# The phase ahead of the selective scans: transposes of delta*u relabelled to the next slot, dt broadcast by a one-row matmul, buffers and waits placed anew

## The chip, the core and the metric

The kernel runs on one core of a Trainium2 chip. The metric is the device time of one execution in microseconds. Before the change three runs took 3381.05, 3383.88 and 3386.18 us; the median is 3383.88 us.

## What is computed

A two-layer decoder over x of 4 batches x 512 tokens x 256 channels. Only the start of layer 0 matters here, a Mamba block on the normalised input, followed by attention, cross-attention and mixtures of experts that the change does not touch:

```python
def mamba_block(x, ...):                      # x: (4, 512, 256), already layer-normed
    residual = x
    xn = rmsnorm(x, norm_m_w)
    x_ssm, z = split(xn @ in_proj_w.T)        # 512 channels each
    x_ssm = silu(causal_depthwise_conv4(x_ssm) + conv_b)
    ssm_p = x_ssm @ x_proj_w.T                # 33 columns: B (16), C (16), dt (1)
    Bp, Cp, dt_raw = ssm_p[:16], ssm_p[16:32], ssm_p[-1:]
    delta = softplus(dt_raw @ dt_w.T + dt_b)  # 512 channels from one column
    A = -exp(A_log)
    y = selective_scan(x_ssm, delta, A, Bp, Cp, D_skip)   # 16 states, over 512 tokens
    return residual + (y * silu(z)) @ out_proj_w.T
```

## The kernel before

Five engines run their own instruction lists and meet at semaphores: PE (matmul), DVE (vector), ACT (scalar functions), POOL (GpSimd) and SP, which issues most DMAs. The order on each engine is written out by hand. SBUF is one tensor, `arena`, so the profile names nearly every buffer `arena`; buffers are laid over one another by `take(..., at=...)`.

Ahead of the main loop over the batches (`Fori(0, B)`) stands a phase that prepares all four batches. It is a software pipeline of six slots, s = 0 to 5. In slot s the stage b1 = s does the layer norm and the RMS norm of a batch (mean, squares, variance, two Sqrts, two rows broadcast by matmuls, `hb` and `a_xn`); the stage b2 = s - 1 does eight in_proj tiles (`in_tile`, four for the conv, four for z), the conv (one ACT operation and three `taps` on DVE for each of four chunks) and the silus to `a_z` and `a_ut`; the stage b3 = s - 2 does x_proj (33 rows into bank 6), the copy to `a_bc`, four small transposes for B, delta, u times delta on POOL (`a_du`), its transposes on PE and their copies to `a_duT` on ACT. SP stores the results of each stage in DRAM and, before the loop, loads those of batch 0 back (`ld_scan`: bT, dl, duT; `ld_late`: ut, zs, xln, xb).

The lines touched, by the numbers of the kernel before: SP 409 to 460 (constants, then x of batch 0 at 420; the dt row stored with C at 425 and loaded back to all partitions at 427; the stores of `keep`; the loads at 454 and 460; `a_kept` at 457); PE 596 to 645 (x_proj ahead of the mean; transposes of `a_du` at 644); ACT 1251 to 1302 (aneg by Exp at 1256, squares 1266, conv 1271, Sqrt 1275 and 1277, Exp 1281, Ln 1284, silus 1289 and 1295, copies 1300, wait on `a_kept`); DVE 1559 to 1647 (constants from 1568; a_bc 1593, centring 1597, taps 1586, dt products 1627, -|x| at 1631, hb 1636, xn 1640, delta 1646); POOL 2150 to 2159 (two stores of zeros that wait for the constants, then delta*u).

The softplus is max(x, 0) + ln(1 + exp(-|x|)). Line 1631 makes -|x| on DVE, lines 1281 and 1284 follow on ACT.

In the loop each batch starts with 16 scans of the state: ACT makes diagonal matrices of B (1314) and dA (1323), PE makes the input term (688), DVE scans (1679), POOL multiplies by C (2167), and PE adds up y (696). The first diagonals wait for `a_kept` in batch 0.

## Time and profile before

| | |
|---|---|
| median of 3 runs | 3383.88 us |
| the profiled execution | 3386.66 us, span 3384.9 us |
| PE busy | 84% of the span, mean granted clock 0.889 |
| DVE / ACT / POOL busy | 46% / 33% / 20% |
| first scan's first matmul | at 210.6 us |
| chain that ended last | PE 69%, DVE 15%, ACT 7%, issue 5%, DMA 2%, POOL 2% |

The profile is of one execution. Times are in microseconds from the span's start, unless marked ns. A row of the timeline gives start, duration, engine, line, operation, output and input, the number of instructions, and in brackets the idle time before the first and what ended it; instructions that follow closely are merged in one row. PEclk is the clock that PE was granted, as a share of 2.4 GHz: 0.5 is 1.2 GHz. A float32 matmul shows as two instructions, so a tile of `in_proj` (two matmuls of 128x512) is four. Rows of the chain of waits give start, duration and what the end of the program waited for in that time.

### The profile page before, as it was taken

The numbers are of one execution on the slowest core, as the hardware profiler recorded it, in microseconds if no ns is written. First come the engines' busy times: TensorE is split into PE (matmuls) and PEld (weight loads), VectorE is DVE, ScalarE is ACT, GpSimd is POOL, SyncE is SP. The second block draws the span as 40 slices with busy tenths as digits, with TensorE's granted clock in tenths as the row PEclk, the third lists the DMA queues.
The fourth block names the chain that finished last, engine by engine and source line by source line (L and its number), as shares of the span: only waits on it lengthen the run. The fifth ranks groups of instructions, "written<-read, shape, count | busy, mean of one in ns | idle before, by whom it ended". The sixth has DMA issues, their size and how long they took to land.

```text
span 3384.9 us, 47651 instructions
## 1 busy us (share of the span) xinstructions
PE 2856.0 (84%) x16822; PEld 1667.4 (49%) x16862; DVE 1558.6 (46%) x2519; ACT 1131.8 (33%) x1943; POOL 686.0 (20%) x370
## 2 busy tenths in 40 slices
PE   6769998999899989996897877878788887589997
PEld 3355425642564356432786524523523532368886
DVE  4555366636663567355011561452453344453443
ACT  3564255425442444242232332333233234111111
POOL 0154054405450446044002000000000000012222
PEclk9779998999899989997898788788688779689999
DMA  5340003000300030004784000000100100224542
GB/s 227 143 157 20 1 1 117 20 1 1 113 24 1 1 109 28 1 0 157 258 296 168 14 1 26 13 1 13 26 0 13 26 1 7 87 92 135 170 148 81
DMA packets 64527, 228.15 MB, mean 67 GB/s; under 512 B 12764, under 2 KB 28788, under 8 KB 46808
## 3 DMA queue, kind: packets, MB, share of 16 engines
q1 hardware_dynamic: 46152, 188.44, 15.6%
q0 software_dynamic: 9984, 20.06, 2.4%
q10 hardware_dynamic: 8208, 17.14, 1.4%
q8 instruction: 124, 2.03, 0.3%
q14 instruction: 59, 0.48, 0.0%
HBM read 180.64 MB, written 40.77 MB: 65 GB/s over the span
## 4 chain that ended last, share of the span: by engine, by line
PE 69%; DVE 15%; ACT 7%; issue 5%; DMA 2%; POOL 2%; ACTq 0%; DVEq 0%; another core or an unknown queue 0%; SPq 0%; POOLq 0%
PE psum L549 35%; PE psum L688 7%; PE psum L915 3%; PE psum L1018 3%; DVE arena L1942 2%; ACT arena L1399 2%; PE psum L696 2%; DVE arena L1759 2%; PE psum L1074 2%; PE psum L864 2%; PE psum L836 2%; PE psum L1087 2%; PE psum L1055 1%; PE psum L567 1%; DVE arena L1743 1%
## 5 line engine op out<-in xcount | busy, mean ns | idle before, releaser
L549 PE MATMUL psum<-arena 128*128 128x512 f32 (+7 forms) x4816 | 1292.2, 420 | 97.2 <-ACT arena L1239 25.7
L549 PEld LDWEIGHTS psum<-arena 128*128 128x128 f32 (+1 forms) x4816 | 814.4, 202 | 515.7 <-issue 363.3
L2167 POOL TENSOR_TENSOR arena<-arena 128x1024 f32<-128x1024 f32 x128 | 299.3, 2372 | 143.6 <-DVE arena L1679 140.1
L1679 DVE TENSOR_TENSOR_SCAN arena<-arena,psum 128x512 f32<-128x512 f32 x256 | 291.3, 1201 | 55.7 <-PE psum L688 55.5
L2204 POOL DMA_INDIRECT arena<-xn,arena x36 | 35.5, 985 | 1205.8 <-DVE arena L2103 1151.9
L688 PEld LDWEIGHTS psum<-arena 128*128 128x128 f32 x2048 | 241.1, 197 | 72.3 <-DVE arena L1679 43.7
L688 PE MATMUL psum<-arena 128*128 128x128 f32 x2048 | 252.0, 283 | 27.6 <-ACT arena L1314 27.6
L2174 POOL TENSOR_TENSOR arena<-arena 128x1024 f32<-128x1024 f32 x32 | 75.9, 2372 | 673.6 <-ACT arena L1399 673.6
L1942 DVE TENSOR_REDUCE arena<-psum 128x1 f32<-128x512 f32 x256 | 160.9, 685 | 100.1 <-PE psum L1055 94.1
L1497 ACT ACTIVATE arena<-psum 128x1024 f32<-128x1024 f32 x128 | 129.9, 1023 | 218.5 <-PE psum L1077 218.5
L1759 DVE SCALAR_TENSOR_TENSOR arena<-psum,arena 128x1024 f32<-128x1024 f32 x128 | 156.9, 1245 | 80.4 <-PE psum L825 80.1
L1399 ACT ACTIVATE arena<-arena 128x1024 f32<-128x1024 f32 x128 | 146.7, 1146 | 112.3 <-DVE arena L1759 112.2
L1525 ACT ACTIVATE arena<-psum 128x256 f32<-128x256 f32 x128 | 49.1, 384 | 385.3 <-PE psum L549 385.3
L1323 ACT ACTIVATE arena<-arena 128x512 f32<-128x512 f32 x256 | 162.8, 708 | 0.1
L2178 POOL TENSOR_TENSOR arena<-arena 128x1024 f32<-128x1024 f32 x64 | 151.2, 2363 | 6.4 <-ACT arena L1399 1.7
L836 PE MATMUL psum<-arena 128*64 128x512 f32 x512 | 138.2, 618 | 14.8 <-ACT arena L1399 6.8
L825 PE MATMUL psum<-arena 64*128 64x512 f32 x512 | 142.5, 638 | 2.7 <-ACT arena L1377 2.7
L1743 DVE RECIPROCAL arena<-arena 128x256 f32<-128x256 f32 x64 | 110.9, 1743 | 46.3 <-ACT arena L1391 46.3
L1055 PE MATMUL psum<-arena 128*128 128x512 bf16 x244 | 95.1, 433 | 37.0 <-DVE arena L1942 35.4
L1239 ACT ACTIVATE arena<-arena 128x512 f32<-128x512 f32 x56 | 33.5, 627 | 254.5 <-DVE arena L1536 138.8
L1018 PE MATMUL psum<-arena 128*128 128x512 bf16 x372 | 93.2, 401 | 21.8 <-DVE arena L1934 15.7
L2127 DVE TENSOR_TENSOR arena<-arena,psum 128x256 f32<-128x256 f32 x128 | 54.0, 422 | 112.1 <-ACT arena L1525 112.1
(286 smaller groups left out, 3186.5 us busy)
## 6 DMA issues: line engine op xcount, KB each, us to landing
arena<-in_W SPq DMA_DIRECT2D x48, 1024.0 KB
arena<-c_rows SPq DMA_DIRECT2D x32, 512.0 KB, 3.8
arena<-in_Wg SPq DMA_DIRECT2D x16, 1024.0 KB, 4.9
arena<-in_Wu SPq DMA_DIRECT2D x16, 1024.0 KB, 7.5
arena<-in_Wd SPq DMA_DIRECT2D x16, 1024.0 KB, 9.8
arena<-dl_all SPq DMA_DIRECT2D x5, 1024.0 KB, 5.1
arena<-duT_all SPq DMA_DIRECT2D x5, 1024.0 KB, 7.5
arena<-ut_all SPq DMA_DIRECT2D x5, 1024.0 KB, 9.2
```

The source lines that it names most:

```text
L549: r = mm(dst, w, x, start=i == 0, stop=i == len(pairs) - 1)
L688: r = mm(bank[4 + c][:, q * P:(q + 1) * P], duT[:, q, c * P:(c + 1) * P], diag[n % 2][:, q, :], start=True, stop=True)
L836: i = mm(bank[0][64 * r:64 * r + 64, :], v1[:, kc, 2 * hp + r, :], t2[u % TBUFS][:, r, :], start=kc == 0, stop=kc == NC - 1)
L1018: r = mm(t[0:SR], select[j][:, h % 8, :], parts[j][:, h // 8, :], start=j == 0, stop=j == 2)
L1323: A_(dA[n % 2][:, c, :], dl[:, c, :], ACT.Exp, scale=aneg[:, c, n:n + 1]).then_inc(dA_ready.sem, 1)
L1399: A_(t2[u % TBUFS], rl[u % RBUFS], ACT.Square, scale=0.125, bias=vec[:, V_NB:V_NB + 1])\
L1679: V.tensor_tensor_scan(hs[n % 3][:, c, :], dA[n % 2][:, c, :], bank[4 + c], 0.0, ALU.mult, ALU.add)\
L1743: V.reciprocal(d, d).then_inc(den_inv.sem, 1)
L1759: V.scalar_tensor_tensor(rl[u % RBUFS], t, minus_nb8, bound[:, kc, :].unsqueeze(1).broadcast_to([P, 2, L]), ALU.max, ALU.min).then_inc(rel ...
L1942: V.reduce_max(negm1[:, qc, h:h + 1], t, AX.X, negate=True).then_inc(s1_max.sem, 1)
L2167: nc.gpsimd.tensor_tensor(h, h, c_all[:, n % CBUFS, :].unsqueeze(1).broadcast_to([P, 2, L]), ALU.mult)\
L2178: nc.gpsimd.tensor_tensor(t, t, t2[kc], ALU.add).then_inc(tsum_step.sem, 1)
```

## The change

- Slots: a fourth stage, b4 = s - 3, takes the transposes of delta*u, their copies and the store of duT. They are the first thing in a slot for PE, ACT and SP; that of the last batch comes after the slots.
- dt: the row stays in `a_bc[32]`; a matmul with a row of ones spreads it over 128 partitions of bank 6, and the dt products read it from there. The store of the row and the load back are gone.
- -|x| on DVE is gone; ACT makes |x| (Abs) and Exp with scale -1.
- Orders: on PE x_proj comes after the mean and the first in_proj tile; on ACT the fourth conv comes after both Sqrts; on DVE the dt products come ahead of taps 2 and both roots follow taps 2; on SP the load of x for batch 0 comes ahead of the constants and the store of dl ahead of that of ut.
- Start: POOL's zero stores and PE wait only for the memsets; constants are waited for later; aneg is made at the end of slot 1.
- End: the wait on `a_kept` (all stores done) is replaced by waits on those stores whose buffers are written next; two of them stand in the loop. Buffers are moved for this: `a_du`, `a_ex`, `a_conv` and `a_z` lie elsewhere, duT of the last batch has a buffer of its own, over xc and sq, and the centring of the last batch waits for the store of duT of batch 0.

```diff
 SP
-            for dst, src in ((const, "consts"), (vec, "vecs")):
-                sp.dma_start(dst, A[src]).then_inc(ld_const.sem, 16)
             sp.dma_start(a_x[0], batch("xT", 0)).then_inc(a_ld_x.sem, 16)
+            for dst, src in ((const, "consts"), (vec, "vecs")):
+                sp.dma_start(dst, A[src]).then_inc(ld_const.sem, 16)
+            def store_duT(b):
+                sp.wait_ge(a_soft.sem, a_soft.at(4 * KI, b))
+                sp.wait_ge(a_st_duT.sem, a_st_duT.at(16, b))
+                sp.dma_start(stored(duT_all, b), a_duT[b == B - 1].rearrange("p a b -> p (a b)")).then_inc(a_st_duT.sem, 16)
...
-                    sp.dma_start(c_rows[b3], a_bc[NS:2 * NS + 1, :]).then_inc(a_st_c.sem, 16)
-                    sp.wait_ge(a_st_c.sem, a_st_c.at(16, b3))
-                    sp.dma_start(a_dt, c_rows[b3, NS:NS + 1, :].broadcast_to([P, L])).then_inc(a_ld_dt.sem, 16)
...
+                if 0 <= b4:
+                    store_duT(b4)
...
-            for s0 in (a_st_c, a_st_xln, a_st_zs, a_st_ut, a_st_dl, a_st_duT):
+            for s0 in (a_st_c, a_st_xln, a_st_zs, a_st_ut):
                 sp.wait_ge(s0.sem, s0.at(0, B))
-            sp.sem_inc(a_kept.sem, 1)
             sp.wait_ge(a_in.sem, a_in.at(0, B))
+            sp.wait_ge(a_turned.sem, a_turned.at(3, B - 1))
+            sp.wait_ge(a_dur.sem, a_dur.at(0, B - 1))
             for dst, src in ((ut, ut_all), (zs, zs_all)):
                 sp.dma_start(dst.rearrange("p a b -> p (a b)"), stored(src, 0)).then_inc(ld_late.sem, 16)
+            store_duT(B - 1)
 PE
+                if 0 <= b4:
+                    turn_du(b4)
                 if b1 < B:
...
-                    for m in range(2):
-                        in_tile(b2, m)
+                    in_tile(b2, 0)
+                if 0 <= b3:
+                    wa(a_gate, 8 + KI, b3)
+                    if b3 >= 1:
+                        wa(a_soft, 4 * KI, b3 - 1)
+                    acc(bank[6][0:33], [(w_xp[:, k, :], a_ut[b3 % 2][:, k, :]) for k in range(KI)]).then_inc(a_turned.sem, 1)
+                if 0 <= b2 < B:
+                    in_tile(b2, 1)
                 if 0 <= b3:
                     wa(a_delta, 1, b3)
+                    mm(bank[6], ones1[32:33, :], a_bc[32:33, :], start=True, stop=True).then_inc(a_turned.sem, 1)
 ACT
-                        wa(a_delta, c + 7, b3)
-                        A_(a_ex[:, c, :], a_ex[:, c, :], ACT.Exp).then_inc(a_soft.sem, 1)
+                        wa(a_delta, c + 3, b3)
+                        A_(a_ex[:, c, :], a_dl[:, c, :], ACT.Abs).then_inc(a_soft.sem, 1)
+                        wa(a_soft, 2 * c + 1, b3)
+                        A_(a_ex[:, c, :], a_ex[:, c, :], ACT.Exp, scale=-1.0).then_inc(a_soft.sem, 1)
...
+                if s == 1:
+                    A_(aneg, vec[:, V_AL:V_AL + KI * NS].rearrange("p (a b) -> p a b", a=KI), ACT.Exp).then_inc(c_exp.sem, 1)
+            take_duT(B - 1)
+            act.wait_ge(c_made.sem, 2)
+            wa(a_delta, 0, B)
-            act.wait_ge(a_kept.sem, 1)
 DVE
+                    if b1 == B - 1:
+                        wa(a_st_duT, 0, 1)
...
+                    for c in range(KI):
+                        V.tensor_scalar(a_dl[:, c, :], bank[6], vec[:, V_DTW + c:V_DTW + c + 1], vec[:, V_DTB + c:V_DTB + c + 1],
+                                        ALU.mult, ALU.add).then_inc(a_delta.sem, 1)
                 if 0 <= b2 < B:
-                    taps(b2, 0)
-                    taps(b2, 1)
+                    taps(b2, 2)
...
-                    for c in range(KI):
-                        wa(a_delta, c + 3, b3)
-                        V.scalar_tensor_tensor(a_ex[:, c, :], a_dl[:, c, :], -1.0, a_dl[:, c, :], ALU.mult, ALU.min)\
-                            .then_inc(a_delta.sem, 1)
```

## Rows read from the trace of the kernel before

**Rows 1.** Windows by slot: length, busy (instructions) by engine, PEclk, DMA share, GB/s
```profile
53.93:94.73 40.80, 29.62 (x96) 14.59 (x96) 22.91 (x36) 20.62 (x31) 6.24 (x4) 0.83 0.31 118
94.73:137.66 42.93, 32.50 (x96) 15.95 (x96) 22.91 (x36) 21.22 (x32) 6.24 (x4) 0.78 0.43 168
137.66:173.89 36.23, 24.65 (x60) 10.18 (x60) 18.41 (x26) 18.26 (x27) 6.24 (x4) 0.78 0.31 125
173.89:210.60 36.71, 11.06 (x28) 4.41 (x29) 9.89 (x14) 13.25 (x21) 6.23 (x4) 0.55 0.38 145
```

**Rows 2.** Timeline of ACT in slots 1 to 4
```profile
51.71 2.17 ACT L1295 ACTIVATE arena<-arena 128x512 f32<-128x512 f32 x4
...
82.85 1.28 ACT L1284 ACT_TABLE_LOAD   x1
...
113.17 0.78 ACT L1271 ACTIVATE arena<-psum,arena 128x512 f32<-128x512 f32 x1 [2.73 <-PE psum L549]
...
123.33 2.44 ACT L1281 ACTIVATE arena<-arena 128x512 f32<-128x512 f32 x4 [5.56 <-DVE arena L1631]
...
162.02 1.28 ACT L1284 ACT_TABLE_LOAD   x1
```

**Rows 3.** Windows of PE alone: length, busy, PEclk, DMA share, GB/s
```profile
54.00:58.00 4.00, 4.00 (x6) 0.63 0.91 377
...
97.00:102.00 5.00, 5.00 (x8) 0.57 0.71 292
```

**Rows 4.** Timeline of PE: last tiles of slot 1, x_proj to tile 1 of slot 2
```profile
45.85 5.33 PE L549 MATMUL psum<-arena 128*128 128x512 f32 x12
53.93 10.47 PE L549 MATMUL psum<-arena 128*33 128x512 f32 x20 [2.76 <-ACT arena L1295]
```

**Rows 5.** Chain of waits in the last slot
```profile
174.67 6.18 PE psum L549 x8
...
184.49 3.31 DMA arena<-c_rows
187.83 1.92 DVE arena L1627 x4
...
190.39 2.44 ACT arena L1281 x4
192.84 1.28 ACT L1284
194.13 0.73 ACT arena L1284
...
203.72 3.90 DMA duT_all<-arena
207.90 1.28 ACT L1314
```

**Rows 6.** POOL in the scans of batch 0; the issue of the C rows, us to landing
```profile
218.03 74.43 POOL L2167 TENSOR_TENSOR arena<-arena 128x1024 f32<-128x1024 f32 x32 [16.13 <-DVE arena L1679]
...
arena<-c_rows SPq DMA_DIRECT2D x2, 512.0 KB, 8.7
```

**Rows 7.** Chain of waits at the start; DMA issue of the constants, us to landing
```profile
1.97 8.61 DMA arena<-in_xT
...
arena<-in_consts SPq DMA_DIRECT2D x1, 616.5 KB, 6.3
```

**Rows 8.** Groups by line and shape, 0 to 210: taps, products, -|x|, centring
```profile
L1586 DVE SCALAR_TENSOR_TENSOR arena<-psum,arena 128x511 f32<-128x511 f32 x16 | 11.9, 743 | 2.4 <-ACT arena L1271 2.4
...
L1631 DVE SCALAR_TENSOR_TENSOR arena<-arena 128x512 f32<-128x512 f32 x16 | 10.0, 687 | 0.0
...
L1627 DVE TENSOR_SCALAR arena<-arena 128x512 f32<-128x512 f32 x16 | 7.6, 542 | 5.5 <-DMA arena<-c_rows 5.5
L1597 DVE TENSOR_TENSOR arena<-arena,psum 128x512 f32<-128x512 f32 x8 | 5.1, 684 | 9.7 <-PE psum L549 9.7
```

**Rows 9.** Waits of SP, 0 to 250: what it waited for, us, times, longest
```profile
SPq L452 <- DMA duT_all<-arena: 7.0, 1, 7.0
```

More of the change, by code:

```diff
@@ L151, in decoder_program @@
         xb = take(KD, L)
+        xc_at = top[0]
         xc = take(KD, L)
@@ L635, in _ @@
                         in_tile(b2, m)
[L636 to L645 removed]
+            turn_du(B - 1)
             wa(a_soft, 0, B)
@@ L1253, in _, with take_conv, take_duT @@
                     act.dma_start(dst, A[src]).then_inc(s.sem, 16)
-            act.wait_ge(ld_const.sem, 32)
             act.wait_ge(c_made.sem, 1)
-            A_(aneg, vec[:, V_AL:V_AL + KI * NS].rearrange("p (a b) -> p a b", a=KI), ACT.Exp).then_inc(c_exp.sem, 1)
-            act.wait_ge(c_made.sem, 2)
             def wa(s, n, b):
                 act.wait_ge(s.sem, s.at(n, b))
-            for s in range(B + 2):
-                b1, b2, b3 = s, s - 1, s - 2
+            def take_conv(b, c):
+                wa(a_in, c + 1, b)
+                if b >= 1:
+                    wa(a_gate, 2 * KI + c + 1, b - 1)
+                tap = V_CW + DCONV * c + DCONV - 1
+                A_(a_conv[:, c, :], bank[c], ACT.Identity, scale=vec[:, tap:tap + 1], bias=vec[:, V_CB + c:V_CB + c + 1])\
+                    .then_inc(a_gate.sem, 1)
+            def take_duT(b):
+                for c in range(KI):
+                    wa(a_turned, c + 4, b)
+                    A_(a_duT[b == B - 1][:, :, c * P:(c + 1) * P], bank[6 + c % 2].rearrange("p (q x) -> p q x", q=NC),
+                       ACT.Identity).then_inc(a_soft.sem, 1)
+            for s in range(B + 2):
+                b1, b2, b3, b4 = s, s - 1, s - 2, s - 3
+                if 0 <= b4:
+                    if b4 >= 1:
+                        wa(a_st_duT, 0, b4)
+                    take_duT(b4)
                 if b1 < B:
@@ L1266, in _ @@
                         A_(sq[:, k, :], xc[:, k, :], ACT.Square).then_inc(a_roots.sem, 1)
+                if s == 0:
+                    act.wait_ge(ld_const.sem, 32)
                 if 0 <= b2 < B:
-                    for c in range(KI):
-                        wa(a_in, c + 1, b2)
-                        tap = V_CW + DCONV * c + DCONV - 1
-                        A_(a_conv[:, c, :], bank[c], ACT.Identity, scale=vec[:, tap:tap + 1], bias=vec[:, V_CB + c:V_CB + c + 1])\
-                            .then_inc(a_gate.sem, 1)
+                    for c in range(3):
+                        take_conv(b2, c)
                 if b1 < B:
@@ L1591, in _ @@
+                if 0 <= b2 < B:
+                    taps(b2, 0)
                 if 0 <= b3:
                     wa(a_turned, 1, b3)
+                    wa(a_st_c, 0, b3)
                     V.tensor_copy(a_bc[0:33, :], bank[6][0:33, :]).then_inc(a_delta.sem, 1)
-                if b1 < B:
-                    wa(a_stats, 1, b1)
-                    for k in range(KD):
-                        V.tensor_tensor(xc[:, k, :], a_x[b1 % 2][:, k, :], bank[4], ALU.subtract).then_inc(a_norm.sem, 1)
+                if 0 <= b2 < B:
+                    taps(b2, 1)
@@ L1611, in _ @@
                     V.tensor_tensor(a_var, a_var, a_r0, ALU.mult).then_inc(a_norm.sem, 1)
-                if 0 <= b2 < B:
-                    taps(b2, 2)
-                if b1 < B:
                     wa(a_roots, 4, b1)
```

163 lines of the change are left out of this document (83 added, 80 removed).

## Prediction

> **What bounds the kernel now.** I read the time by stages first, since the change touches only what lies ahead of the first scan. The phase ends when the first scan's weights start on PE at 210.60, 6% of the span. It runs in six slots; PE finished the transposes of delta*u at 94.73, 137.66 and 173.89, so the inner slots last 40.8, 42.9 and 36.2 us, the last one with what follows it 36.7 [rows 1]. In none is an engine full: of 42.93 us PE is busy 32.50, DVE 22.91, ACT 21.22, and PE's clock is 0.78. So a slot is a chain through all engines, and the chain of waits must be read, not the busy shares.
>
> The chain in an inner slot: x_proj on PE (a_ut from the slot before), the mean, in_proj tiles, the fourth conv on ACT (113.17), Sqrt, taps, dt products and -|x| on DVE, Exp only at 123.33 [rows 2], Ln, silus, copies of the transposed delta*u. PE begins each slot at half clock: 0.63 in 54 to 58, 0.57 in 97 to 102 [rows 3]. The tiles at full clock cost 5.33 us for three, 1.73 us back to back [rows 4]; at half clock 3.4.
>
> The last slot, with no tiles beside it, is bare: x_proj 6.18, then the dt row goes to DRAM and back (the load alone 3.31), DVE starts only at 187.83, 7 us after x_proj's end, Exp at 190.39; the last copy ends at 203.70, its store takes 3.90, ACT is let on at 207.90 [rows 5]. The scans of batch 0 are then paced by POOL, which is busy without a gap from 218.03 for 74.43 us; its start is the landing of the first C rows, 8.7 us after their issue at 209.44 [rows 6]. PE's own scan chain is only about 2 us ahead of it, so both have to start earlier for a gain.
>
> **What the change leaves alone.** "One slot later" moves nothing on PE or ACT: transposes and copies were last in slot s and become first in slot s+1, with the same neighbours, except that x_proj no longer follows at once. I give that relabelling zero. It is the other edits that can pay. The arithmetic of the scans and all later stages are the same; the two waits that move into the loop (on the dl and duT stores) are met by then: the dl store is issued some 4 us ahead of the last copy, and scan n=1 comes 10 us behind that copy.
>
> **Part by part,** in time order, against the profiled execution (3386.66 us, span 3384.9).
>
> Slot 0. x lands at 10.58, 8.61 us after its issue, third in SP's queue behind 616.5 KB of constants that took 6.3 us [rows 7]. Now it is first, issued at about 1.05. 512 KB at the constants' rate would land at about 6.6. But POOL's zero stores (3.7 MB) no longer wait for constants and start some 7 us earlier beside it: I take 7.2, a gain of 3.3 us (0 if they take the whole share, 4.0 if none). The constants, now later, are needed only by Sqrt and the row matmuls, some 6 us after x; no cost.
>
> Slot 1. Conv 3 moves behind both Sqrts. The r0 chain on DVE no longer waits for it, but taps 3 come after. With taps of three dependent operations, 0.75 each [rows 8], taps 2 ends at 41.4, r0 at 42.1, second Sqrt 42.5, conv 3 43.3, taps 3 45.7, xn 48.3, last tile 49.6 (before 45.85 + 5.33 = 51.2 [rows 4]), silus 52.0 (before 51.71 + 2.17 = 53.9 [rows 2]). Gain 1.8. The aneg exponential with its table load, 1.5 us, now ends at 53.6 and holds back the squares of slot 2 by 0.9; this is in the next figure.
>
> Slot 2. Before, x_proj, mean and two tiles ran from 53.93 to 64.40 [rows 4], 20 instructions, a third of them at half clock. Now mean and tile 0 need only xn, so PE goes on without a stop and x_proj finds a_ut done: mean 51.3, tile 53.0, x_proj 56.5, tile 1 58.2, all at full clock. DVE: taps 0 57.8, a_bc 58.5; PE one-row matmul (two instructions, 0.86) and four transposes to 59.9; taps 1 61.3; four dt products from PSUM. No row has these from PSUM: from SBUF they take 542 ns; the nearest rows with PSUM, the centring, take 684 ns [rows 8]. I take 0.65 each, 2.6 us (ends 2.2 and 2.8). By the Trainium skill (VectorE: DVE Perf Modes, Why PSUM operands drop a tier) a float32 operand in PSUM falls to the one-element rate; that speaks against the move, and would be 533 ns a product plus overhead, inside my ends. Products end 64.2, taps 2 66.5, the two roots 67.4, conv 3 68.3, taps 3 70.6, xn 73.2, last tile 74.5. ACT then has a table load of 1.28 and four pairs of Abs and Exp. Abs isn't in the trace; I take it as a Square, 0.63, with a dependent Exp 0.71: 5.4 us against 2.44 before. It replaces four DVE products at 687 ns [rows 8]. Abs starts near 69.6, Exp ends 75.0 (the next table load came at 82.85 before [rows 2]); Ln, silus and copies keep their spacing: from Exp's end (82.85) to the end of the transposes (94.73) were 11.9 us. Transposes end at 87.0 against 94.73: 7.7 for slots 1 and 2.
>
> Slot 3. Here PE starts cold again behind the transposes: mean and tile 0 at half clock, 6.8, x_proj at full 10.3, tile 1 12.0. A new wait enters: DVE's centring of the last batch waits for the delta*u store of batch 0, which SP issues at the start of the same slot; that store took 7.0 us in SP's wait [rows 9]. So centring 8.1 to 9.4, squares and conv 0 10.8, taps 0 13.1, a_bc 13.8, one-row matmul and transposes 15.1, taps 1 16.1, products 18.9, taps 2 21.2, roots 22.0, conv 3 22.9, Abs from 22.9 + 1.28. Before, conv 3 ended at 19.2 and Exp began at 28.6 in this slot. Queued behind the wait on DVE: taps 0, the a_bc copy, so PE's one-row matmul. Abs/Exp end at 29.6 against 31.0: gain 1.4; the wait costs 0.8 of it.
>
> Slot 4. No norm: tile 0 3.4, x_proj 7.6, a_bc 8.4, PE 10.6, products 15.3, conv 3 14.9, Abs from 16.3 to 21.6 against the table load at 162.02 [rows 2], 24.3 into the slot: gain 2.7.
>
> Slot 5. x_proj and copy end 7.7 into the slot, as before. Then PE at half clock: two instructions 1.7, transposes 0.43; B copy; first product at 10.8 where it was 13.9 + 0.5. Abs 0, then the Exp table, which before was loaded during the wait and now stands between Abs and Exp, 1.28; pairs end at 17.5, against 18.95. Gain 1.4, of the 7 us that the DRAM trip held. By the Trainium skill (ScalarE: Activation LUTs, What ACT_TABLE_LOAD costs) a switch costs 2.66 us with a drain; here Ln starts 1.29 us after the load does [rows 5], so the row decides; by the page the gain here would be 0.
>
> Tail. ACT no longer waits for the last store: 4.1 us (203.72 to 207.90) [rows 5]. For POOL the C rows must follow. SP now queues dl store, ut, zs from 4 us ahead of the last copy, then the duT store, then C at 1.2 us behind it. That is 4 MB ahead of C; at 1 MB in 2.6 us it lands about 9.8 us behind the copy, where it was 14.3. POOL gains 4.5, PE 4.1; 4.1 stands.
>
> Sum: 3.3 + 7.7 + 1.4 + 2.7 + 1.4 + 4.1 = 20.6 us. Profiled: 3366.1. The median of the three runs lies 2.8 us lower, 3383.88, so the forecast is 3363.3.
>
> **The rivals.**
> A, PE stays cold. I grant full clock to slot 2 throughout and after 7 us in slot 3. If x_proj and one tile of slots 2, 3 and 4 run at half clock as in [rows 3], each loses 2 to 3.5: 8 us, gain 12, 3372. For it: PE's idle in the slots grows where ACT gets 3 us more. Chance 0.12.
> B, the start of the scans is held by transfers: 4 MB ahead of C, landing as late as before; POOL's 4.5 is lost, gain 16, 3368. Inside the forecast's range; chance 0.12.
> C, slower. Abs isn't in the set of tables that holds Exp; then Abs and Exp alternate with a load each time, six more per slot at 1.28, 7.7 us in each of four slots, on ACT where the chain is: +30.8, 3394. It decides from four extra loads per slot (5.1 us, a quarter of the gain). Against it: Square and Identity follow Silu, Sqrt and Ln without a load in the trace. The Trainium skill (ScalarE: Activation LUTs, Table sets: the hidden batching unit) has abs in every set, which would rule it out. Chance 0.04.
> D, more is won: the slots' front is limited less than I think (DVE order, cold clock gone), 28 to 36 us, 3352. Chance 0.10.
> E, a new wait or a drift of later stages swallows it, within 0.2%: 0.05. A further 0.01 for slower by other ways.
> Forecast 0.56.
>
> **How the numbers follow.** 0.2%, 6.8 us, is about what a measurement of this kernel can tell from no change. Faster needs under 3377: forecast, A, B and D, 0.90; same 0.05; slower 0.05. The range takes in A, B and most of D: gains of 10 to 31, 3353 to 3374.
>
> **What would show it.** First PE instruction near 7.3; transposes of slots 2 to 4 ending near 83.7, 125, 159 (before 94.7, 137.7, 173.9); four table loads per slot and no more; centring of slot 3 released by the duT store; first scan matmul near 190; POOL's first product near 198. Wrong would be: extra table loads, PE's first instruction at 10 or later, POOL starting over 9 us behind PE, or the slots at 42 us as before.

## The result and the profile after

The kernel after takes 3407.20 us (median of 5 runs, 3399.29 to 3409.93) against 3383.88 (5 runs, 3379.38 to 3390.47): ratio 1.0061, interval 1.0045 to 1.0076. It is slower by 23 us where 20 us were forecast as won. The profiled execution takes 3409.93 us, its span is 3408.2, PE's mean granted clock 0.880 (0.889 before).

The first view to read is not the page but a comparison of milestones. From the scans on, ACT's table loads are the same and in the same order in both traces, so each gives a shift. Where the scans of batch 0 begin, the kernel after is 11.26 us ahead (table load at 196.64, before 207.90). At the last load of the program it is 22.94 us behind (3334.04, before 3311.10). So the phase that was changed gained, and 34.2 us were lost in stages of which no line was touched. Of the two numbers the gain is the softer: in four traces taken later of kernels that have the phase of the kernel before line for line (b_stall, b_pe6, b_pe18, b_dve7 below) this load comes at 202.98, 203.34, 204.98 and 207.60, so 207.90 is at the late end of 5 us of scatter.

The windows of the kernel after by slot (length, then busy time and instructions of PE, PEld, DVE, ACT and POOL, granted clock, DMA share, GB/s) answer to [rows 1]:

```profile
57.49:92.16 34.67, 26.80 (x95) 13.61 (x94) 21.37 (x32) 24.73 (x39) 6.23 (x4) 0.87 0.34 131
92.16:137.42 45.26, 35.14 (x100) 17.67 (x99) 21.82 (x32) 23.27 (x36) 6.25 (x4) 0.76 0.38 153
137.42:169.87 32.45, 25.32 (x63) 9.97 (x61) 17.14 (x22) 20.41 (x31) 6.24 (x4) 0.82 0.32 131
169.87:199.35 29.48, 11.47 (x30) 4.38 (x31) 9.62 (x11) 15.52 (x25) 6.24 (x4) 0.56 0.44 168
```

Slot 4 and what follows are shorter than before, slot 3 is longer (45.26 against 42.93) although PE's idle time in it is 10.1 us where it was 10.4: PE is simply slower there, at a clock of 0.76.

Slot 0 is read from the timeline of ACT of the kernel after. ACTq rows are the weight loads that ACT issues:

```profile
5.80 0.60 ACTq L1269 DMA_DIRECT2D arena<-in_down_w  x1
6.43 2.01 ACTq L1269 DMA_DIRECT2D arena<-in_xWq  x1
8.47 2.59 ACTq L1269 DMA_DIRECT2D arena<-in_xWk  x1
11.09 2.77 ACTq L1269 DMA_DIRECT2D arena<-in_xWv  x1
13.88 1.74 ACTq L1269 DMA_DIRECT2D arena<-in_xWo  x1
15.65 1.63 ACTq L1269 DMA_DIRECT2D arena<-in_gate_W  x1
17.31 1.84 ACTq L1269 DMA_DIRECT2D arena<-in_gate_b  x1
19.24 1.28 ACT L1297 ACT_TABLE_LOAD   x1 [19.24 <-issue]
```

x is there early, as intended (PE begins at 7.83, before 10.72), but the squares need ACT, and ACT is still issuing. Before, all sixteen issues were done at 9.4, at some 0.5 us each. Here the last six take 1.6 to 2.8 us each. The first in_proj tile of batch 0 starts at 33.72 where it started at 27.16.

The stages behind the phase give the rest. In this table a number is the time between two of ACT's table loads in one execution: from the first Exp of the self-attention to the gate's Silu in layer 0 (four batches); from the shared expert's Gelu to the next Sqrt in layer 1, which holds the turn of y (three batches); and the stretch with the attention of layer 1 (four batches).

| | layer-0 attention | turn of y | layer-1 attention |
|---|---|---|---|
| before | 51.8, 51.8, 56.7, 53.5 = 213.8 | 41.4, 42.9, 42.2 = 126.5 | 104.8, 103.0, 103.0, 103.0 = 413.8 |
| after | 57.0, 57.2, 57.2, 57.0 = 228.3 | 43.9, 44.7, 43.8 = 132.5 | 108.4, 103.0, 108.4, 109.3 = 429.1 |

That is 14.5 + 6.0 + 15.3 = 35.8 us; everything else together is some 1.5 us shorter.

What happens in the layer-0 attention of batch 0, first in the kernel before. These are timeline rows of DVE and PE (L1720 is the second normalisation of the attention's output, L756 the transposes of the next probabilities), then, in a fence of their own, windows, in which the clock is the third number from the end:

```profile
341.23 0.43 DVE L1720 TENSOR_TENSOR arena<-psum,arena 128x256 f32<-128x256 f32 x1 [1.39 <-PE psum L549]
...
342.88 0.55 PE L756 MATMUL psum<-arena 128*128 128x128 f32 x3 [0.75 <-ACT arena L1354]
343.26 2.55 PE L549 MATMUL psum<-arena 128*128 128x64 f32 x10
```

```profile
343.00:345.00 2.00, 2.00 (x12) 1.50 (x13) 0.60 (x2) 0.67 (x2) 0.00 (x0) 1.00 0.02 4
345.00:347.00 2.00, 2.00 (x9) 0.71 (x8) 0.08 (x1) 0.00 (x0) 0.00 (x0) 1.00 0.00 0
```

The same timelines and then windows of the kernel after:

```profile
334.17 0.43 DVE L1759 TENSOR_TENSOR arena<-psum,arena 128x256 f32<-128x256 f32 x1 [1.74 <-PE psum L558]
...
335.82 0.90 PE L772 MATMUL psum<-arena 128*128 128x128 f32 x3 [1.10 <-ACT arena L1389]
336.51 4.90 PE L558 MATMUL psum<-arena 128*128 128x64 f32 x10
```

```profile
335.28:337.28 2.00, 1.46 (x8) 1.46 (x8) 1.23 (x3) 1.16 (x4) 0.00 (x0) 0.60 0.00 0
337.28:339.28 2.00, 2.00 (x5) 1.19 (x6) 0.04 (x1) 0.00 (x0) 0.00 (x0) 0.50 0.01 4
339.28:341.28 2.00, 2.00 (x3) 0.34 (x1) 0.00 (x0) 0.00 (x0) 0.00 (x0) 0.50 0.00 0
```

DVE's normalisation comes 0.35 us later after the same releaser (1.74 against 1.39), PE's pause 1.65 us on is 1.10 instead of 0.75, and then PE runs at half clock for most of 6 us: ten matmuls take 4.90 us instead of 2.55. The idle of 1.39 stands in all four batches of the kernel before, 1.74 to 1.76 in all four of the kernel after.

The length of the whole stretch goes with the clock. Windows over the stretches of batches 0, 2 and 3 of the kernel before:

```profile
322.26:374.08 51.82, 47.43 (x229) 28.01 (x230) 18.95 (x44) 17.29 (x46) 0.00 (x0) 1.00 0.00 1
1007.36:1064.11 56.75, 52.36 (x229) 30.56 (x230) 18.95 (x44) 17.29 (x46) 0.00 (x0) 0.91 0.00 1
1355.10:1408.55 53.45, 49.06 (x229) 28.78 (x230) 18.94 (x44) 17.30 (x46) 0.00 (x0) 0.97 0.00 1
```

and of batch 1 of the kernel after:

```profile
661.06:718.22 57.16, 52.43 (x229) 30.52 (x230) 18.93 (x44) 17.30 (x47) 0.00 (x0) 0.91 0.00 1
```

The same 229 matmuls take 51.8 us at a mean clock of 1.00, 53.5 at 0.97 and 57 at 0.91. In the kernel after the mean is 0.91 in all four batches: PE is at half clock for 10.2 us of each, in pieces that begin some 2, 22 and (in two batches) 46 us into the stretch. The pause of 1.10 is the one ahead of the piece that begins at 22 us. In the kernel before batch 2 has this pattern too, although its pause is 0.75; the other three have the first piece at most.

And the turn of y in layer 1, batch 1, in the timeline of PE, before:

```profile
2106.92 1.96 PE L943 MATMUL psum<-arena 128*128 128x128 f32 x8 [4.27 <-issue]
```

and after:

```profile
2116.71 0.90 PE L959 MATMUL psum<-arena 128*128 128x128 f32 x3 [4.72 <-issue]
2119.76 1.23 PE L959 MATMUL psum<-arena 128*128 128x128 f32 x5 [2.15 <-issue]
```

Eight transposes that wait for nothing between one another are cut into three and five, with 2.15 us in which PE "waits for nothing that the profile shows". The two later batches have the same cut, with 2.18 and 2.15.

### The profile page after: what moved, and what is told of

It is laid out like the page before. It is cut to its first block, busy times and chain, and to the rows that moved or that the text cites. A ratio compares the mean times of both kernels' runs of the same rounds, so it can differ in the third digit from the quotient of the medians.

```text
span 3408.2 us, 47711 instructions
## 1 busy us (share of the span) xinstructions
PE 2881.0 (85%) x16830; PEld 1674.7 (49%) x16870; DVE 1554.6 (46%) x2503; ACT 1141.6 (33%) x1960; POOL 686.2 (20%) x370
## 3 DMA queue, kind: packets, MB, share of 16 engines
q1 hardware_dynamic: 45632, 187.38, 15.3%
## 4 chain that ended last, share of the span: by engine, by line
PE 69%; DVE 14%; ACT 7%; issue 5%; DMA 2%; POOL 1%; ACTq 1%; DVEq 0%; another core or an unknown queue 0%; SPq 0%; POOLq 0%
PE psum L558 34%; PE psum L704 7%; PE psum L931 3%; PE psum L1034 3%; DVE arena L1981 2%; PE psum L712 2%; PE psum L1090 2%; ACT arena L1434 2%; DVE arena L1798 2%; PE psum L880 2%; PE psum L852 2%; PE psum L1103 2%; PE psum L1071 2%; PE psum L576 1%; DVE arena L1782 1%
## 5 line engine op out<-in xcount | busy, mean ns | idle before, releaser
L558 PE MATMUL psum<-arena 128*128 128x512 f32 (+6 forms) x4816 | 1297.9, 422 | 98.6 <-ACT arena L1255 25.7
L558 PEld LDWEIGHTS psum<-arena 128*128 128x128 f32 x4816 | 818.7, 204 | 519.2 <-issue 361.2
L704 PEld LDWEIGHTS psum<-arena 128*128 128x128 f32 x2048 | 242.1, 198 | 68.3 <-DVE arena L1718 42.8
L704 PE MATMUL psum<-arena 128*128 128x128 f32 x2048 | 252.9, 284 | 23.9 <-ACT arena L1348 23.9
```

The costliest lines, as they stand in the source:

```text
L558: r = mm(dst, w, x, start=i == 0, stop=i == len(pairs) - 1)
L704: r = mm(bank[4 + c][:, q * P:(q + 1) * P], duT[:, q, c * P:(c + 1) * P], diag[n % 2][:, q, :], start=True, stop=True)
```

## The experiments

Two questions: what costs 34 us in unchanged code, and where 9 of the 20 us of the phase ahead went. Ratios are to runs of the kernel before on the same chip. The texts on record call the candidates by letters: T1, the later stages suffer because the loop starts at another time; S1, slot 0 is lost to POOL's early stores; D and P, the place of DVE's or PE's code matters. By an instruction's place I mean the number of instructions ahead of it in its engine's compiled list. PE's loop body is unchanged; DVE's has one of the two new waits (at the second scan), which adds no instruction to the trace: the shift is 7 at the loop's start and 7 in the attention. But the phase ahead of the loop is longer: the loop begins at place 174 before and 181 after on DVE, at 260 and 266 on PE, at 164 and 195 on ACT. The traces, which record nearly every instruction, have 171 and 178 ahead of it on DVE, 161 and 192 on ACT, but 793 and 811 on PE: there the difference is 18, not 6.

### The start shifted, nothing else

b_hold2 and b_hold5 delay the kernel before by two and five operations on ACT; a_hold2 delays the kernel after by two. (They move ACT's loop by a few places as well; b_act31 below shows that this is harmless.)

```diff
+            for i in range(2):        # b_hold5: 5
+                act.wait_ge(c_exp.sem, i + 1)
+                A_(logits1..., const[:, 0:CH * E1], ACT.Identity).then_inc(c_exp.sem, 1)
             with act.Fori(0, B) as b:
```

> The kernel before, with two dependent Identity operations of 128x256 (about 0.45 us each) put on ACT ahead of its loop, so that the loop starts about 0.9 us later and nothing else changes. Theory T1 (the PE clock falls in the attention parts by the time at which these begin, so a shift of the loop's start changes how often it falls): the self-attention stretch of a batch, 51.8 us in batches 0 and 1 of the kernel before and 57 in all batches of the changed one, takes one of these two lengths by the shift; the total moves by more than the hold, by up to 30 us, in either direction. T2 (the changed kernel is slower in the loop since its code or its buffers lie elsewhere, or by the two waits moved into the loop): the stretches stay at 51.8, 51.8, 56.8, 53.5 and the total grows by 0.9 us to about 3385.

> The same with five operations, a hold of about 2.3 us. T1: with the loop's start moved by this much, the first self-attention begins at a place that in the changed kernel gave 57 us; so 57 us in at least the first two batches and a total 10 to 30 us over the kernel before, 3395 to 3410. T2: stretches as before, 3386.

> The changed kernel with the same hold of 0.9 us ahead of ACT's loop. T1: self-attention of 51.8 us in some or all batches, and a total 10 to 30 us under the changed kernel's 3407, so 3376 to 3396, although work was added. T2: 57 us in all batches as in the changed kernel, 3408.

Measured: b_hold2 3387.91 us, ratio 1.0003 (0.9993 to 1.0012); b_hold5 3388.24, 1.0009 (0.9999 to 1.0020); a_hold2 3405.16, 1.0060 (1.0042 to 1.0077). The four attention stretches are 53.5, 51.8, 53.4, 51.8 and 53.4, 53.5, 53.4, 51.8 in the two made from the kernel before, and 57.2, 57.1, 57.1, 57.2 in the third. As the cause of the 57 us T1 falls: the kernel after keeps them in every batch wherever the start lies. The stretches of the kernel before do scatter between 51.8 and 56.7 from batch to batch and execution to execution, and what starts it in one batch and not in another is not shown.

### POOL's stores of zeros in slot 0

```diff
+            pool.wait_ge(ld_const.sem, 32)
             pool.wait_ge(c_made.sem, 1)
```

> The changed kernel, but POOL's two stores of zeros wait for the constants again. It separates the loss in slot 0: there ACT's sixteen weight loads took until 19.2 us to issue instead of 9.4, and the first squares came at 20.5. Theory S1 (POOL's early stores fill the DMA queues and hold ACT's issues): issues end near 10, slot 0 ends near 24 and the first scan matmul comes near 189.5 instead of 199.35. Rival S2 (the order x, constants on SP does it): issues stay at 19 and the scans at 199. The total is 3397 if the loop is unchanged; by T1 it may lie anywhere from 3370 to 3400.

Measured: 3399.79 us, ratio 1.0043 (1.0028 to 1.0057), 5.8 us nearer to the kernel before than a_hold2's ratio; 3397 was expected. Timeline of ACT:

```profile
5.98 0.66 ACTq L1269 DMA_DIRECT2D arena<-in_xWq  x1
...
9.75 0.54 ACTq L1269 DMA_DIRECT2D arena<-in_gate_b  x1
11.80 1.28 ACT L1297 ACT_TABLE_LOAD   x1 [11.80 <-DVE arena L1622]
```

The issues are short again and the first table load comes at 11.80, not 19.24; the scans' table load comes at 183.62, 13.0 us earlier than in the kernel after, of which 10.1 are left at the end of the profiled executions (3399.79 against 3409.93). SP's order, x ahead of the constants, is the same in both, so the order is not the cause; S1 is shown. The attention stretches stay at 57.0 to 57.2, so the loss behind the phase is a matter of its own.

### The place of the code on three engines

Here the kernel before gets what the kernel after has in places, as waits that are met at once: 7 on DVE and 6 on PE just ahead of the loop, 31 on ACT in the last slot, where it idles. In the opposite direction the kernel after gets 121 on DVE, so that its loop stands 128 places behind that of the kernel before. (Two waits of the source make one instruction; the traces of b_dve7, b_pe6, b_act31 and a_dve121 have 7, 6, 31 and 121 more than the kernel that they were made from.)

```diff
+            for _ in range(14):        # b_pe6: 12 on PE; b_act31: 62 on ACT; a_dve121: 242 on DVE
+                dve.wait_ge(a_kept.sem, 1)
             with dve.Fori(0, B) as b:
```

> The kernel before, with seven more wait instructions on DVE (on a semaphore that has long come) just ahead of its loop, where DVE sits idle. Nothing else changes, but the loop's code on DVE now stands as far from the start as in the changed kernel, 7 instructions further. Theory D (the place of the code: in the changed kernel DVE's second normalisation of the attention output starts 0.36 us later than its inputs allow, PE's gap grows from 0.75 to 1.1 us, its clock falls, and the stretch takes 57.1 us instead of 51.8 or 53.5): the self-attention stretch takes 57 us in all four batches and the total is near the changed kernel's loss, 3405 to 3415 (before plus 20 to 30). Rival E (something else of the change does it): stretches of 51.8 to 53.5 and a total of 3385.

> The kernel before, with six more wait instructions on PE ahead of its loop, which moves PE's loop code by as much as the change does. Theory D: no effect, 3385, stretches 51.8 to 53.5. Rival P (it is PE's code that matters): 57 us stretches, over 3400.

> The kernel before, with 31 more wait instructions on ACT in the last slot, where ACT is idle; ACT's loop code stands where it does in the changed kernel. Theory D: no effect, 3385. Rival A (ACT's code): 57 us stretches, over 3400.

> The changed kernel, with 121 more wait instructions on DVE just ahead of its loop, where DVE waits some 8 us for PE; its loop's code then stands 128 instructions further than in the kernel before. Theory D, if the effect repeats after 128 instructions: the stretches fall back to 51.8 to 53.5 and the total to 3372 to 3380, under the kernel before by what the phase ahead of the scans gained (11 us). If the waits take longer than the 8 us, a few more. Rival E: 57 us and 3407 or more.

Measured: b_dve7 3399.71 us, ratio 1.0036 (1.0024 to 1.0048); b_pe6 3387.24, 0.9998 (0.9986 to 1.0009); b_act31 3386.80, 1.0008 (0.9997 to 1.0019); a_dve121 3393.94, 1.0023 (1.0009 to 1.0036). Seven idle waits on DVE cost the kernel before 12 us, less than the 20 to 30 expected. a_dve121 missed its 3372 to 3380: it wins 13 us over the kernel after, by the ratios, but stays above the kernel before. Timeline of DVE in b_dve7 at the second normalisation:

```profile
341.39 0.43 DVE L1722 TENSOR_TENSOR arena<-psum,arena 128x256 f32<-128x256 f32 x1 [1.74 <-PE psum L549]
```

and in a_dve121:

```profile
333.54 0.43 DVE L1761 TENSOR_TENSOR arena<-psum,arena 128x256 f32<-128x256 f32 x1 [1.39 <-PE psum L558]
```

So the 0.35 us come with DVE's place and go with it, in all four batches of each, and the attention stretches with them (55.5, 57.2, 57.1, 57.2 in b_dve7; 53.4, 53.4, 51.8, 51.8 in a_dve121). The two profiled executions are extremes of their ten, 3407.35 the slowest and 3385.51 the second fastest, so these lengths flatter the contrast; the idle time does not depend on that. It is 1.74 to 1.76 in every batch of the four kernels whose loop stands 7 places further on (the kernel after, a_hold2, a_pool, b_dve7), and 1.39 in every batch of the twelve others with 0, 64 or 128 places (b_stall, below, is late by work).

The trace also shows where the 0.35 us are: in the kernel after and in b_dve7, 446 recorded instructions of DVE stand ahead of the wait before this normalisation, and the normalisation starts 0.42 us after the wait; in the kernel before 439 stand ahead and it starts 0.07 us after. PE's result was there, and the profile names nothing else that the instruction waits for.

### PE's place, and how often the places repeat

b_pe6 had not reproduced the cut in the turn of y. But an f32 matmul of 512 columns is one entry of the compiled list and two weight loads and two matmuls in the trace (the one-row matmul of slot 5 stands at 177.30 and again at 177.84). Four of them are three places more each, so what the kernel after really adds on PE is 6 + 12 = 18, which is the 811 less 793 of the traces.

```diff
+            for _ in range(36):        # b_pe18; a_dve57: 114 on DVE of the kernel after
+                pe.wait_ge(c_made.sem, 1)
             with pe.Fori(0, B) as b:
```

> The kernel before with 18 wait instructions that are met at once put on PE ahead of the batch loop, so that PE's later instructions lie as many places further on as in the kernel after (there: two more waits net of what is gone, and four one-row f32 matmuls, which the trace shows as two weight loads and two matmuls each). Theory P (the place of PE's code costs time in layer 1): the eight transposes of the layer-1 loop at the turn of y, one row of 1.96 us in the kernel before, are split into 3 and 5 with some 2.2 us of idle by issue between them, as in the kernel after, and the stretch around them is 2 to 3 us longer in each of three batches: 3390 to 3393 us. Rival (the gap comes from the instructions or addresses of the kernel after, not from PE's place): one row of 1.96 us, time as before, 3383 to 3388.

> The kernel after with 57 wait instructions that are met at once put on DVE ahead of the batch loop: the loop's first instruction stands at 238 instead of 181, which is 64 places behind the 174 of the kernel before; 121 such waits (128 places behind 174) had brought the layer-0 attention stretches from 57 to 52 and 53 us. If what matters repeats every 64 instructions: stretches of 51.8 to 53.5 us and 3388 to 3396 us. If it repeats only every 128: stretches of 57 us or some other number, and 3400 to 3408 us.

Measured: b_pe18 3400.63 us, ratio 1.0036 (1.0024 to 1.0049). Timeline of PE in b_pe18:

```profile
2108.02 0.90 PE L945 MATMUL psum<-arena 128*128 128x128 f32 x3 [4.79 <-issue]
2111.07 1.23 PE L945 MATMUL psum<-arena 128*128 128x128 f32 x5 [2.15 <-issue]
```

and in b_pe6:

```profile
2106.04 1.97 PE L945 MATMUL psum<-arena 128*128 128x128 f32 x8 [5.22 <-issue]
```

The cut is between the same two transposes as in the kernel after. Its stretches of the turn are 44.1, 44.3 and 44.6. The cut is there in all three batches of every kernel whose PE loop stands 18 places further on (six traces, 1.88 to 2.59 us by issue) and in none of the eleven others with 0, 6, 64 or 128. P is shown. The total missed its 3390 to 3393: the medians differ by 10 us, the three stretches by 6.4 only; the layer-1 attention of b_pe18 took 423.9 where the kernel before had 413.8.

a_dve57 took 3396.86 us (3388 to 3396 expected), ratio 1.0013 (0.9999 to 1.0027), with the normalisation's idle at 1.39 in all batches and stretches of 56.5, 53.5, 53.5, 51.8. A shift of 64 places restores DVE as well as one of 128.

### All repaired

a_place takes the kernel after, with POOL's wait of a_pool, the 121 waits on DVE and 110 on PE (18 + 110 = 128). a_best takes a_place and drops the wait of slot 3 (one more wait as filling keeps DVE's loop in its place). Dropping it is allowed: duT of batch 0 leaves from another buffer than the one that the centring writes.

```diff
                 if b1 < B:
                     wa(a_stats, 1, b1)
-                    if b1 == B - 1:
-                        wa(a_st_duT, 0, 1)
                     for k in range(KD):
```

> The kernel after with three edits: POOL's stores of zeros wait for the constants (slot 0 repaired), 121 met waits on DVE and 110 met waits on PE ahead of the batch loop, so that the loop code of both stands 128 places behind that of the kernel before. Theory (the loss in the later stages is the place of the code of DVE and PE): layer-0 attention stretches 52 to 53.5 us, no gap inside the eight transposes of the layer-1 turn of y, the loop starts near 184 us instead of 208 and nothing is given back: 3362 to 3372 us. Rival (something else in the kernel after slows the later stages too, the ACT's place or the stores): 3378 to 3390 us.

> As the run before it, and slot 3 of the phase ahead of the scans no longer holds DVE's centring for the duT store of batch 0; the places of the loop code are the same. If that wait costs slot 3 its time (centring released 13.9 us late, then PE at half clock): slot 3 falls from 45 to some 41 us, PE's row of conversions there is at the full clock, and the run is 2 to 5 us faster than the one before it. If the slot was bound by another chain anyway: within 1 us of it.

Measured: a_place 3382.79 us, ratio 0.9971 (0.9960 to 0.9981); a_best 3374.71, 0.9955 (0.9943 to 0.9968). In both the attention stretches are 51.8 to 53.5 and the eight transposes of the turn of y are whole. Slot 3, counted between the last copies of two batches, takes 45.7 us in a_place and 37.6 in a_best: dropping the wait is worth 8 us, more than the 2 to 5 I expected. In a_pool, which has the same wait, slot 3 took 42.7 us, so its price is 5 to 8, by how long PE's clock then stays low. But a_place missed its 3362 to 3372, and the timeline of PE in a_best shows the largest part of it:

```profile
191.27 8.98 PE L706 MATMUL psum<-arena 128*128 128x128 f32 x56 [11.05 <-issue]
```

The waits used as filling are not free: 110 of them stood between PE and the first scan, and the trace has them 0.11 us apart. PE idles 11.05 us there where it idles 3.36 in a_pool, so they delay the first scan by 7.7 us.

### The filling out of the way

a_best2 moves the waits to the start of the program. a_best3 uses 57 on DVE there and 46 on PE (18 + 46 = 64) between the one-row matmul of slot 5 and the last transposes.

```diff
+            for _ in range(92):        # a_best3; a_best2: 221, ahead of slot 0
+                pe.wait_ge(c_made.sem, 1)
             turn_du(B - 1)
```

> The fastest kernel so far (POOL's stores of zeros wait for the constants, no wait for the duT store in slot 3, loop code of DVE and PE 128 places behind that of the kernel before), with the met waits on DVE and PE moved from just ahead of the batch loop to the start of the program, where both wait for the first input. If the first scan was late there because DVE worked off 121 waits (POOL's first product was released by DVE 18.4 us after ACT's scan table load began, where the kernel after has 11.5), POOL's first product comes 3 to 6 us earlier: 3366 to 3372 us, every later stage the same. Rival: the first products wait for the C rows or the scan's loads anyway: within 1 us of the fastest, 3373 to 3376 us; or the start of the program is now late by the waits: the same or slower.

> The repairs of the fastest kernels so far (POOL's stores of zeros wait for the constants; no wait for the duT store in slot 3), with fewer met waits and in idle stretches: 57 on DVE at the start of the program, where it waits for the first centring, and 46 on PE between the one-row matmul and the last 16 transposes, where it idles 11.9 us. The loop code of DVE and PE then stands 64 places behind that of the kernel before, not 128. In the two kernels with 110 waits on PE these waits took 6 to 11 us of PE's time: at the start the first matmul came at 13.73 instead of 7.2, ahead of the loop PE sat 11.05 by issue. Theory: with them out of the way ACT's scan table load begins near 181, POOL's first product is near 192.5 and PE's gap in the layer-1 turn of y is absent (its place counts in steps of 64 as well): 3362 to 3368 us. Rival (64 places aren't enough for PE): the gap of 1.9 to 2.4 us is back in three batches, 3368 to 3374 us.

Measured: a_best2 3370.15 us, ratio 0.9944 (0.9930 to 0.9957). POOL's first product comes 12.3 us behind the scans' table load, where it was 15.7 in a_best (the expectation's 18.4 is the second product, at 199.27 behind a load at 180.88), so 3.4 us earlier, as the theory has it; but PE's first matmul comes at 13.73 instead of 7.41, so the rival holds as well and part of the cost has only moved to the front. a_best3 takes 3365.93 us (3365.01 to 3370.40), ratio 0.9940 (0.9927 to 0.9953): the lowest of all, though the intervals of a_best2 and a_best overlap with it. Timeline of PE in slot 3 and of POOL in a_best3:

```profile
96.00 7.21 PE L558 MATMUL psum<-arena 128*128 128x512 f32 x28
...
192.84 48.93 POOL L2209 TENSOR_TENSOR arena<-arena 128x1024 f32<-128x1024 f32 x21 [13.26 <-DMA arena<-c_rows]
```

POOL's first product was expected near 192.5. The transposes of the turn are whole in all three batches, so 64 places are enough for PE too.

### The step from 0.35 us to 4 us

Only read so far was that the short delay is what takes PE's clock down. b_stall makes the delay by work and leaves every place up to that point as it was (behind it they move by one):

```diff
+                        if qc == 1:
+                            V.tensor_tensor(logits1...[:, 0:256], const[:, 0:256], const[:, 0:256], ALU.mult)
                         V.tensor_tensor(o_nat...
```

> The kernel before with one more operation on DVE in each batch of the layer-0 attention, a product of 128x256 f32 into a tile that is not in use there, right ahead of the second normalisation of the attention's output. No code ahead of the batch loop is touched; DVE's place at this point is as before. It makes that normalisation late by some 0.35 us by work instead of by a stall, as the kernel after has it late by 0.35 us (idle 1.74 instead of 1.39 us). Theory: the delay itself is enough, PE's pause behind it takes PE's clock down, and the four attention stretches take 55 to 57 us instead of 51.8 to 53.5: 3398 to 3408 us against the kernel before. Rival (the delay costs its own length and no more; the 4 us come from something else that goes with DVE's place): stretches at most 1 us longer, 3384 to 3392 us.

Measured: 3401.25 us, ratio 1.0038 (1.0027 to 1.0049), and all four stretches 57.1 us. Timelines of DVE and PE in b_stall:

```profile
338.84 0.42 DVE L1721 TENSOR_TENSOR arena<-arena 128x256 f32<-128x256 f32 x1 [1.39 <-PE psum L549]
339.18 0.42 DVE L1723 TENSOR_TENSOR arena<-psum,arena 128x256 f32<-128x256 f32 x1
...
340.82 0.80 PE L756 MATMUL psum<-arena 128*128 128x128 f32 x3 [1.09 <-ACT arena L1354]
341.41 4.01 PE L549 MATMUL psum<-arena 128*128 128x64 f32 x10
```

and a window of b_stall:

```profile
341.00:343.00 2.00, 2.00 (x10) 2.00 (x10) 0.56 (x1) 0.67 (x2) 0.00 (x0) 0.50 0.00 0
```

The normalisation starts 0.34 us later, PE's pause is 1.09 instead of 0.75, the clock falls to 0.50, and the kernel before turns into something as slow in these stretches as the kernel after (228.5 against 228.3 us over four batches; the mean clock of each is 0.91). The rival, that the delay costs its own length and no more, falls. Four operations that each delay what follows by 0.34 us, 1.4 us in all, cost 12 us.

## Why the prediction was wrong

**"The arithmetic of the scans and all later stages are the same."** This step failed, and with it the sign. The arithmetic is the same, the time is not: 34.2 us, of which 14.5 lie in the layer-0 attention, 6.0 in the turn of y and 15.3 in the layer-1 attention, with some 1.5 won elsewhere. The first is DVE's place (b_dve7 makes it, a_dve121 and a_dve57 undo it) by way of PE's clock (b_stall); the second is PE's place (b_pe18 makes it, a_place and a_best3 undo it). I had given "a drift of later stages" 0.05 under rival E, with no mechanism and no size. The trace of before could have suggested both: its attention stretches already scatter between 51.8 and 56.7 with identical work, at mean clocks of 1.00 to 0.91, so PE stood close to a fall of its clock there, and its rows carry idle times "by issue".

The Trainium skill has a figure for this (Advanced Engine Details and Errata, ISA Cache): the cache for an engine's code has lines of 256 instructions. If only the ends of such lines mattered, a shift of 64 or 128 places would not put DVE's loop back where it was; measured, both bring the idle of 1.39 back, so here 64 is a period (or a part of 64 is), and the measurement decides.

**The sum, term by term** (gains in us, measured from the ends of the last transposes of each slot):

| | forecast | measured |
|---|---|---|
| slot 0 | 3.3 | -6.6 |
| slots 1 and 2 | 7.7 | 9.1 |
| slot 3 | 1.4 | -2.3 |
| slot 4 | 2.7 | 3.8 |
| slot 5 | 1.4 | 3.0 |
| tail | 4.1 | 4.2 |
| sum | 20.6 | 11.2 |

The measured column is one execution against one; as said above, that of the kernel before is a late one.

*Slot 0.* The term counted what POOL's early stores take from the load of x, and that was nearly right (PE at 7.83, forecast 7.3). It left out who else uses the queues: six of ACT's sixteen weight issues became three to six times as long, and the squares stand behind them on ACT. a_pool shows it. The bound "0 if they take the whole share" was no bound, since it looked at the transfer and not at the engine that issues.

*Slots 1 and 2.* Right in mechanism. The dt products from PSUM took 0.74 each, 2.96 us for four, above the 2.2 to 2.8 I had set:

```profile
67.62 2.96 DVE L1647 TENSOR_SCALAR arena<-psum,arena 128x512 f32<-128x512 f32 x4
...
74.17 0.62 ACT L1315 ACTIVATE arena<-arena 128x512 f32<-128x512 f32 x1
74.81 1.28 ACT L1317 ACT_TABLE_LOAD   x1
76.11 0.63 ACT L1317 ACTIVATE arena<-arena 128x512 f32<-128x512 f32 x1
76.64 0.61 ACT L1315 ACTIVATE arena<-arena 128x512 f32<-128x512 f32 x1
...
77.82 0.61 ACT L1315 ACTIVATE arena<-arena 128x512 f32<-128x512 f32 x1
```

(kernel after, DVE and ACT, slot 2). The cost was smaller on ACT: a pair of Abs and Exp repeats every 1.18 us. Abs follows Exp with no load between, so rival C has no support in any slot.

*Slot 3.* The wait on the store of duT was seen, with its release at the right place; its price was not. Kernel after, timelines of DVE and PE:

```profile
100.93 1.28 DVE L1622 TENSOR_TENSOR arena<-arena,psum 128x512 f32<-128x512 f32 x2 [13.85 <-DMA duT_all<-arena]
...
106.53 0.79 PE L635 MATMUL psum<-arena 1*128 1x512 f32 x1 [4.81 <-DVE arena L1636]
...
108.11 13.35 PE L558 MATMUL psum<-arena 128*128 128x512 f32 x28
```

I charged 0.8 us for the delay and nothing for what PE does behind it. PE idles 4.81 us, then the same 28 matmuls take 13.35 us at a clock of 0.50 (window 112 to 119) where a_best3, without the wait, has them in 7.21. From a_place to a_best the slot shrinks by 8 us, from a_pool to a_best by 5. This is rival A in one slot, brought about by a wait that I had priced without it.

*Slot 5.* Gained 3.0, not 1.4: the pairs of Abs and Exp took 6.13 us from the first Abs to the next table load (179.56 to 185.69, ACT), 0.6 less than I had, and the chain up to the first product was shorter as well. In the rows above, too, the Exp starts 1.30 after its table load does; the Trainium skill's 2.66 us a switch (ScalarE: Activation LUTs, What ACT_TABLE_LOAD costs) is not what this trace shows, as before.

*Tail.* ACT goes on at 196.64 right behind the last copy (4.2 won, forecast 4.1). POOL's first product comes at 208.09, released by the C rows 11.5 us behind the copy, where I had 9.8.

**What this adds up to.** With slot 0, slot 3 and the places of the code put right, the same change takes 3365.93 us, 0.6% or some 20 us under the kernel before on its chip. The forecast was 3363.3, but the closeness is partly luck: the scans of a_best3 start 26.5 us earlier than those of the kernel before (181.40 against 207.90), 6 more than forecast (slot 3, without its wait, is 38.78 long where I had 41.5; and up to 5 of the 26.5 are the late execution of the kernel before), and 9.8 us are given back behind them: 3.0 in the layer-0 attention, 5.5 in the layer-1 attention, 2.1 elsewhere, less 0.7 in the turn of y.

**What stays open.** The layer-1 attention cost 15.3 of the 34.2 us. Over four batches it took 412 to 417 us in the kernel before and in the variants of it that leave DVE and PE in place (b_hold2, b_hold5, b_act31, b_stall), 424 in the three that move one of them (b_dve7, b_pe6, b_pe18), 425 to 430 in the kernel after, a_hold2 and a_pool, and 414 to 423 in the six that restore one or both. Here too the length goes with PE's clock. Windows over three stretches of the kernel after (batches 1, 2 and 3):

```profile
2242.36:2345.36 103.00, 78.64 (x363) 20.73 (x368) 53.10 (x102) 37.29 (x40) 0.00 (x0) 0.90 0.02 6
2512.42:2620.87 108.45, 83.29 (x363) 21.65 (x368) 53.27 (x102) 37.29 (x40) 0.00 (x0) 0.86 0.02 5
2785.76:2895.04 109.28, 85.50 (x363) 21.04 (x368) 53.28 (x102) 37.41 (x39) 0.00 (x0) 0.83 0.02 5
```

The work is the same and the mean clock is 0.90, 0.86 or 0.83. In the 68 stretches of the 17 traces PE goes to half clock 4.4 to 4.8 us after the start in all but one of the short ones (103.0 to 104.8 us) and stays there for 17.1 us; in the long ones (108.4 to 109.3) it does so at 7.7 to 7.8 or at 4.1 and stays there for 23.9 or 27.3 us. So the 15.3 us go with the clock, too. What sets that moment is not shown, and the place of the code is not needed for it: b_hold2 has a stretch of 108.4 with both loops in place, b_pe6 has two long ones at an unchanged total. Long ones are 1 in 20 with DVE and PE in place, 14 in 24 with one or both moved, 6 in 24 where one or both are restored; that place has a share in it is likely and not tested by itself.

Nor is it shown what the seven or eighteen places do inside the engine; that code is fetched in pieces of 64 instructions or a part of that is the reading that fits, and "issue" idle is all that the profile says. And it is open why the same pause of 0.75 us lets the clock fall in some batches of the kernel before and not in others.

## What to carry to other kernels

When a change adds or removes instructions ahead of a long loop, compare the untouched stages first, milestone by milestone; an engine that pauses longer behind the same releaser, or a run of matmuls cut in two "by issue", points to the place of the code and not to the work. It can be tested by adding waits that are already met, in a stretch where the engine idles, until the loop stands a multiple of 64 instructions from where it was, counting instructions in the trace, where an f32 matmul of 512 columns is four. Compare the mean granted clock of stretches with the same work before looking for another cause: here it goes with nearly all of the difference. And take more than one trace of the kernel before: its phase ahead of the loop alone scatters by 5 us. Price a new wait by the stretch of half clock that PE's idle brings behind it, and an earlier transfer by the engines whose issues stand in the same queues.

## What the runs showed of the hardware

- Seven more instructions ahead of DVE's loop move a stall of 0.35 us to an instruction that PE waits for; 57 or 121 take it away. Eighteen on PE put 1.9 to 2.6 us between two transposes that depend on nothing new; 64 or 128 take it away.
- A delay of 0.34 us on DVE, which makes PE's pause 1.09 us instead of 0.75, takes PE from 2.4 to 1.2 GHz right behind it. The mean clock of the stretch is then 0.91 in every batch, where it was 1.00, 1.00, 0.91 and 0.97; the price is 3.7 us per batch on average.
- Waits that are met at once are not free: 110 of them on PE follow one another every 0.11 us, 11.7 us in all, and the idle by issue that they leave is 11.05 us.
- ACT's issue of a weight load takes 0.5 us, and 1.6 to 2.8 us when POOL's 3.7 MB of stores are under way beside it, the loads of 8 and 4 KB among them.
